# Attention kernel, two layers: both halves of P·V are copied out by ScalarE and added by GpSimd, instead of one copy and an addition on VectorE

## The chip, the cores and the metric

The kernel runs on one core of one Trainium2 chip. The metric is the device time of one execution in microseconds (us), as the median of the runs. TensorE is written PE (PEld for its weight loads), VectorE DVE, ScalarE ACT, GpSimd POOL, SyncE SP.

## The reference

Two attention layers over a batch of 8 images with 512 channels and T = 32·32 = 1024 positions, all float32; layer 1 has the same form with its own weights.

```python
xn = group_norm(x, w, b)                       # 32 groups
qkv = einsum('oc,bct->bot', qkv_w, xn) + qkv_b # 8 heads of 64 channels
weight = softmax(einsum('bct,bcs->bts', q * scale, k * scale), axis=-1)
a = einsum('bts,bcs->bct', weight, v)
hout = einsum('oc,bct->bot', proj_w, a) + proj_b
return x + hout
```

## The kernel before, in words

To hold float32 accuracy, each operand of a matmul is split into a rounded high part and the rest, the low part (`pt_hi` and `pt_lo`, `a_hi` and `a_lo`, and so on). Products of high and low parts are added up in PSUM.

The program is 16 passes (2 layers by 8 images). A pass has a head of its own (normalised input, queries, keys, values), then 4 **pairs** of heads, then the projection. A pair is 16 **steps** m = 0..15, one for each tile of 128 query rows. The first three pairs are a loop body ("middle pairs"); the last is written apart (`last=True`), since it has no next queries and keys to compute, and PE fills some of its steps with single matmuls of the projection. Every engine has its own instruction list, written out by hand and run in its order; semaphores tie the lists together. Nothing reorders them, so what stands behind a waiting instruction on an engine waits too.

What step m does:

- PE computes the scores of tile m+2 (`ps_s`, L766 and L768), transposes the normalised probabilities of tile m (`ps_t`, L777), computes a piece of the next head's queries and keys (middle pairs, L731), and does half of a **weigh** (`ps_o`, L789 and L790): the product of the values with the transposed probabilities of two tiles. The weigh of group k (k = 0..7) runs in steps 2k+2 and 2k+3; the weigh of group 7 stands behind step 15.
- DVE takes the row minimum of tile m+2 (L575), subtracts to get `pt_lo` of tile m (L584, two halves), and takes the reciprocal of the row sum of tile m+2 (L579).
- ACT copies `pt_hi` of tile m out of `ps_t` (`high_part`, L477, two halves) and computes the exponential of tile m+2 (L472).
- POOL multiplies tile m+2 by the reciprocal (`normalise`, L373), and splits queries, keys, values and weights for what comes next.

PE may transpose tile m only when tile m is normalised and `pt_lo` of tile m-1 is written (`lo_ready`, half by half).

The stationary operand of a weigh holds the high and the low values side by side, so that `ps_o` ends with two halves of 64 partitions that have to be added. ACT copies one half, shifted to the partitions of the other, into `o_part` (`other_half`, L484), and DVE adds it to the half that is still in PSUM, into `attn` (`add_halves`, L593). Groups 0 to 3 give the lower head, 4 to 7 the upper. When groups 4+k are in, `attn` is split: `attn_high(k)` on ACT (L497), `attn_split(k)` on POOL (L400). PE's next weigh waits for `attn_ready`, which says that `ps_o` has been read.

Where these stand: in a middle pair ACT does `other_half` at the start of even steps 4 to 14 and behind the high parts in step 15; in the last pair it stands in odd steps, between the high parts and the exponential. The end of a pair on ACT is `attn_high(2)`, `other_half` of group 7, `attn_high(3)`, and right behind it the high parts of tile 0 of the next pair.

Of the kernel before, what the change touches and what calls it, by code (L numbers as in the profile page):

```python
# [7 lines left out]
F32 = mybir.dt.float32  # L8
F32R = mybir.dt.float32r
I32 = mybir.dt.int32  # L10
ALU = mybir.AluOpType
# [25 lines left out]
LO_CREDIT, SUM_CREDIT, SPLIT_CREDIT, OUT_CREDIT, PV_CREDIT, STORE_CREDIT = 2, 1, 4, 8, 1, 1  # L37
# [10 lines left out]
def build(nc, x, wqk, wv, wp, bqk, bv, bo, nw, nb, consts, out):  # L48
    mid = nc.dram_tensor("layer0_out", (B, C, T), F32, kind="Internal").ap()

    with ExitStack() as ctx:
# [40 lines left out]
        o_part = [sb(f"o_part{s}", [P, GROUP], F32) for s in range(2)]  # L92
        a_hi = sb("a_hi", [P, PAIRS, T], F32R)
# [111 lines left out]
        def sum_at(g):  # L205
            return g + 1 + SUM_CREDIT

# [122 lines left out]
        def _(pool):  # L330
# [51 lines left out]
            nc.gpsimd.memset(scratch[:, 4:6], 0.0).then_inc(a_ready, SPLIT_CREDIT)  # L382
# [9 lines left out]
            split_wqk(1, 1, 0)  # L392

# [8 lines left out]
            def pair_steps(i, p, last):  # L402
                pair = PAIRS * i + p
                tile = TILES * i + PT_STEPS * p
                for e in range(2):
                    hh = 2 * p + e
                    hd = H * i + hh
                    for j in range(NT):
                        m = NT * e + j
                        if j == 1 and not (last and e == 1):  # L410
                            split_qk(hd + 1, 1 - e, 1)
                        if j == 3 and not (last and e == 1):
                            v_low(hd + 1, hh + 1, 1 - e)
                        if e == 1 and j in (5, 7):
                            attn_split(pair, p, (j - 5) // 2)
                        if j == 4 + e and not (last and e == 1):
                            split_wqk(hd + 3, 1 - e, pair + 1 + e)
                        if j == 6 and not last:
                            pool.wait_ge(scores_ready, tile + NT * (e + 1))
                            split_qk(hd + 2, e, 0)  # L420
                        if not (last and m + 2 >= PT_STEPS):
                            normalise(tile + m + 2, m + 2)
                attn_split(pair, p, 2)
                attn_split(pair, p, 3)
# [28 lines left out]
        def _(act):  # L453
# [26 lines left out]
            def other_half(g, k):  # L480

                src, dst = (slice(D, P), slice(0, D)) if k < 4 else (slice(0, D), slice(D, P))
                act.wait_ge(pv_done, pv_at(g))
                nc.scalar.copy(o_part[k % 2][dst, :], ps_o[src, 0:GROUP]).then_inc(part_ready, 1)  # L484
# [86 lines left out]
        def _(dve):  # L571
# [15 lines left out]
            def add_halves(pair, k):  # L587
                rows = slice(0, D) if k < 4 else slice(D, P)
                cols = slice((k % 4) * GROUP, (k % 4 + 1) * GROUP)
                dve.wait_ge(part_ready, 8 * pair + k + 1)  # L590
                if k < 4:
                    dve.wait_ge(a_ready, a_at(pair - 1, k))
                nc.vector.tensor_tensor(attn[rows, cols], ps_o[rows, 0:GROUP], o_part[k % 2][rows, :],  # L593
                                        ALU.add).then_inc(attn_ready, 1)

# [65 lines left out]
            nc.vector.memset(scratch[:, 1:2], 0.0).then_inc(attn_ready, SUM_CREDIT)  # L661
# [18 lines left out]
            def pair_steps(i, p, last):  # L680
                pair = PAIRS * i + p
                tile = TILES * i + PT_STEPS * p
                for m in range(PT_STEPS):
                    if not last and m >= 4 and m % 2 == 0:
                        add_halves(pair, m // 2 - 2)
# [4 lines left out]
                    if m == PT_STEPS - 1 or last and m >= 3 and m % 2 == 1:  # L690
                        add_halves(pair, (m - 3) // 2)
# [10 lines left out]
                add_halves(pair, 7)  # L702
# [24 lines left out]
        def _(pe):  # L727
# [53 lines left out]
            def weigh(tile, g, hd, k, lo, hi):  # L781

                if lo == 0:
                    pe.wait_ge(attn_ready, sum_at(g - 1))
                    pe.wait_ge(v_ready, hd + 1)
                    pe.wait_ge(lo_ready, lo_at(tile + 2 * k + 1, 1))
# [165 lines left out]
```

## Time and profile before

| | |
|---|---|
| median of 3 runs | 4327.01 us (4325.28 to 4327.69) |
| the profiled execution's own time | 4325.15 us |
| its span | 4323.0 us |
| PE busy | 4279.9 us, 99% |
| DVE busy | 3280.7 us, 76% |
| ACT busy | 2915.8 us, 67% |
| POOL busy | 2429.0 us, 56% |
| granted PE clock | 1.00 of full speed |

The profiled execution spends 2.15 us outside its span and lies 1.86 us below the median. A matmul's record includes its passage through the array, so records overlap; the distance from one start to the next tells more than their lengths. The chain of work that ended last gives each matmul only the time by which it moved that chain on.

### The profile page before, as it was taken

Reading aid. Unit: us, or ns where it says so; the run is one execution under the profiler, and the core shown is the slowest. Engines: PE = TensorE matmul, PEld = TensorE weight load, DVE = VectorE, ACT = ScalarE, POOL = GpSimd, SP = SyncE. Lnnn points to the kernel's source line nnn. Section 1 sums busy time; section 2 is a strip of 40 time slices with the busy share of each in tenths; the row PEclk is TensorE's granted clock in tenths of the full one; section 3 lists DMA queues with packets and bytes.
Section 4 is the critical chain, followed back from the end, with each engine's and each line's share of the span. In section 5 each row is a group of like instructions: output and inputs, shape, how many; then the busy total and the mean of one; then the engine's idle time right before and its main releaser. Section 6 shows DMA issues by size and latency. Waiting matters only on the chain.

```text
span 4323.0 us, 89926 instructions
## 1 busy us (share of the span) xinstructions
PE 4279.9 (99%) x26692; PEld 3740.2 (87%) x26692; DVE 3280.7 (76%) x5479; ACT 2915.8 (67%) x5375; POOL 2429.0 (56%) x2332
## 2 busy tenths in 40 slices
PE   8999999999999999999999999999999999999999
PEld 6888888888888888888888888888888888888888
DVE  5777867788686786777867788686886867868787
ACT  4757847577575775757757577575775757667576
POOL 5655556465564655646566465564655646556464
PEclk9999999999999999999999999999999999999999
DMA  3232222322223222232222212222222222222222
GB/s 87 49 96 47 71 72 49 96 47 80 64 47 96 48 79 65 49 94 49 78 74 60 86 45 83 64 63 81 47 81 66 65 79 48 79 64 68 75 49 88
DMA packets 99645, 295.08 MB, mean 68 GB/s; under 512 B 15104, under 2 KB 15232, under 8 KB 99328
## 3 DMA queue, kind: packets, MB, share of 16 engines
q1 hardware_dynamic: 99328, 291.19, 25.0%
q8 instruction: 158, 2.59, 0.2%
q14 instruction: 159, 1.30, 0.1%
HBM read 123.36 MB, written 33.55 MB: 36 GB/s over the span
## 4 chain that ended last, share of the span: by engine, by line
PE 97%; DVE 2%; issue 1%; ACT 0%; DMA 0%; DVEq 0%; POOL 0%; SPq 0%; POOLq 0%
PE ps_t L777 21%; PE ps_g L731 15%; PE ps_o L789 11%; PE ps_o L790 11%; PE ps_s L768 11%; PE ps_s L766 11%; PE ps_s L731 7%; PE ps_t L731 5%; PE ps_o L731 3%; DVE rstd_bits L627 0%; DVE seed L625 0%; DVE pt_lo L584 0%; ACT pt_hi L477 0%; DVE work L631 0%; DVE rstd_bits L632 0%
## 5 line engine op out<-in xcount | busy, mean ns | idle before, releaser
L373 POOL TENSOR_SCALAR probs<-probs,row_rcp 128x1024 f32<-128x1024 f32 x1024 | 1149.5, 1123 | 1371.1 <-DVE row_rcp L579 1371.1
L575 DVE TENSOR_REDUCE row_min<-ps_s 128x1 f32<-128x1024 f32 x1024 | 1250.4, 1221 | 214.4 <-PE ps_s L768 198.9
L477 ACT CAST pt_hi<-ps_t 128x512 fp32r<-128x512 f32 x2048 | 1112.0, 590 | 434.7 <-PE ps_t L777 423.5
L584 DVE TENSOR_TENSOR pt_lo<-ps_t,pt_hi 128x512 fp32r<-128x512 f32 x2048 | 1309.5, 680 | 9.5 <-ACT pt_hi L477 5.0
L472 ACT ACTIVATE probs<-ps_s,row_min 128x1024 f32<-128x1024 f32 x1024 | 1150.7, 1124 | 210.2 <-DVE row_min L575 193.6
L777 PEld LDWEIGHTS ps_t<-const_sb,probs 128*128 128x128 f32 x8192 | 945.2, 140 | 179.5 <-DVE pt_lo L584 49.6
L777 PE MATMUL ps_t<-const_sb,probs 128*128 128x128 f32 x8192 | 1084.1, 274 | 3.6 <-DVE pt_lo L584 3.4
L789 PE MATMUL ps_o<-pt_hi,v_st 128*128 128x256 f32 x4096 | 1044.2, 288 | 0.0
L790 PE MATMUL ps_o<-pt_lo,v_st 128*128 128x256 f32 x4096 | 1014.9, 282 | 0.0
L768 PE MATMUL ps_s<-kl_st,q_st 128*128 128x512 f32 x2048 | 808.7, 395 | 0.0
L766 PE MATMUL ps_s<-kh_st,q_st 128*128 128x512 f32 x2048 | 806.6, 394 | 0.0
L789 PEld LDWEIGHTS ps_o<-pt_hi,v_st 128*128 128x128 f32 x4096 | 771.9, 188 | 38.9 <-issue 12.4
L790 PEld LDWEIGHTS ps_o<-pt_lo,v_st 128*128 128x128 f32 x4096 | 774.6, 189 | 29.1
L768 PEld LDWEIGHTS ps_s<-kl_st,q_st 128*128 128x128 f32 x2048 | 388.1, 190 | 53.8
L593 DVE TENSOR_TENSOR attn<-ps_o,o_part 64x256 f32<-64x256 f32 x512 | 215.8, 421 | 281.2 <-ACT o_part L484 276.2
L766 PEld LDWEIGHTS ps_s<-kh_st,q_st 128*128 128x128 f32 x2048 | 385.9, 188 | 48.6
L731 PE MATMUL ps_g<-xn_hi,wqk_hi 128*128 128x512 f32 x768 | 352.7, 459 | 0.0
L362 POOL TENSOR_TENSOR kl_st<-qk,kh_st 128x512 fp32r<-128x512 f32 x256 | 329.3, 1286 | 21.4
L484 ACT COPY o_part<-ps_o 64x256 f32<-64x256 f32 x512 | 187.6, 366 | 186.4 <-PE ps_o L790 179.4
L731 PE MATMUL ps_g<-xn_hi,wqk_lo 128*128 128x512 f32 x768 | 307.2, 400 | 0.0
L579 DVE RECIPROCAL row_rcp<-row_sum 128x1 f32<-128x1 f32 x1024 | 167.9, 164 | 182.4 <-ACT probs L472 147.8
L400 POOL TENSOR_TENSOR a_lo<-attn,a_hi 128x256 f32 (+1 forms) x256 | 189.8, 741 | 204.3 <-ACT a_hi L497 204.3
(117 smaller groups left out, 4948.7 us busy)
## 6 DMA issues: line engine op xcount, KB each, us to landing
wqk_raw<-in_wqk SPq DMA_DIRECT2D x130, 256.0 KB, 2.6
q_st<-kh_st SPq DMA_DIRECT2D x128, 256.0 KB, 2.9
q_st<-kl_st SPq DMA_DIRECT2D x128, 256.0 KB, 3.6
kh_st<-kh_st SPq DMA_DIRECT2D x128, 256.0 KB, 2.9
kl_st<-kl_st SPq DMA_DIRECT2D x128, 256.0 KB, 3.6
x_raw<-layer_out SPq DMA_DIRECT2D x36, 512.0 KB, 5.3
wv_raw<-in_wv SPq DMA_DIRECT2D x66, 256.0 KB, 4.4
x_raw<-in_x SPq DMA_DIRECT2D x32, 512.0 KB, 5.3
```

Of the source, the lines that this page charges most:

```text
L362: nc.gpsimd.tensor_tensor(kl_st[s][:, cols], qk[:, cols], f32(kh_st[s][:, cols]), ALU.subtract).then_inc(qk_split, 1)
L373: nc.gpsimd.tensor_scalar(probs[m % 2][:, :], probs[m % 2][:, :], row_rcp[:, m % 4:m % 4 + 1], 1.0, ALU.mult, ALU.mult).then_inc(probs_rea ...
L472: nc.scalar.activation(probs[m % 2][:, :], ps_s[:, m % 2, :], ACT.Exp, bias=row_min[:, m % 4:m % 4 + 1], scale=-1.0, accum_out=row_sum[:, ...
L477: nc.scalar.copy(pt_hi[:, m // 2 % 2, 4 * half:4 * half + 4, (m % 2) * P:(m % 2 + 1) * P], ps_t[:, half, :].rearrange("p (b t) -> p b t", ...
L575: nc.vector.tensor_reduce(row_min[:, m % 4:m % 4 + 1], ps_s[:, m % 2, :], AX.X, ALU.min).then_inc(min_ready, 1)
L584: nc.vector.tensor_tensor(pt_lo[place], ps_t[:, half, :].rearrange("p (b t) -> p b t", b=4), f32(pt_hi[place]), ALU.subtract).then_inc(lo_ ...
L731: return nc.tensor.matmul(bank, stat[hi_lo[0]](n // 3), mov[hi_lo[1]](n // 3), start=first, stop=last)
L766: nc.tensor.matmul(ps_s[:, m % 2, cols], q_st[s][:, j * P:(j + 1) * P], kh_st[s][:, cols], start=True, stop=False)
L768: mm = nc.tensor.matmul(ps_s[:, m % 2, cols], q_st[s][:, j * P:(j + 1) * P], kl_st[s][:, cols], start=False, stop=True)
L777: mm = nc.tensor.transpose(ps_t[:, half, b * P:(b + 1) * P], probs[m % 2][:, (4 * half + b) * P:(4 * half + b + 1) * P], ident)
L789: nc.tensor.matmul(ps_o[:, 0:GROUP], v, pt_hi[:, k % 2, b, :], start=(b == 0), stop=False)
L790: mm = nc.tensor.matmul(ps_o[:, 0:GROUP], v, pt_lo[:, k % 2, b, :], start=False, stop=(b == BLK - 1))
```

## The change

ACT now makes two copies for each group: the half that stays on its partitions goes to a new buffer `o_same`, the other to `o_part` as before. POOL adds the two from SBUF into `attn`. PE's next weigh waits for ACT's second copy (`part_ready`), no longer for the addition. DVE's 512 additions are gone; the waits of `attn_high` and `attn_split` for `attn_ready` now wait for POOL.

```diff
+            def add_halves(pair, k):                       # block.gpsimd
+                rows = slice(0, D) if k < 4 else slice(D, P)
+                cols = slice((k % 4) * GROUP, (k % 4 + 1) * GROUP)
+                pool.wait_ge(part_ready, part_at(8 * pair + k))
+                if k < 4:
+                    pool.wait_ge(a_ready, a_at(pair - 1, k))
+                nc.gpsimd.tensor_tensor(attn[rows, cols], o_same[k % 2][rows, :], o_part[k % 2][rows, :],
+                                        ALU.add).then_inc(attn_ready, 1)
+                pool.wait_ge(attn_ready, sum_at(8 * pair + k))
...
                         m = NT * e + j
+                        if m >= 4 and m % 2 == 0:
+                            pool.wait_ge(probs_ready, tile + m + 2)
+                            add_halves(pair, m // 2 - 2)
...
+                if last:
+                    pool.wait_ge(a_ready, a_at(pair, 1))
+                else:
+                    pool.wait_ge(probs_ready, tile + PT_STEPS + 2)
+                add_halves(pair, 6)
                 attn_split(pair, p, 2)
+                pool.wait_ge(a_ready, a_at(pair, 2))
+                add_halves(pair, 7)
                 attn_split(pair, p, 3)
...
             def other_half(g, k):                          # block.scalar
+                act.wait_ge(attn_ready, sum_at(g - 2))
                 act.wait_ge(pv_done, pv_at(g))
+                nc.scalar.copy(o_same[k % 2][dst, :], ps_o[dst, 0:GROUP])
                 nc.scalar.copy(o_part[k % 2][dst, :], ps_o[src, 0:GROUP]).then_inc(part_ready, 1)
...
-            def add_halves(pair, k):                       # block.vector, with its three calls
-                dve.wait_ge(part_ready, 8 * pair + k + 1)
-                nc.vector.tensor_tensor(attn[rows, cols], ps_o[rows, 0:GROUP], o_part[k % 2][rows, :],
-                                        ALU.add).then_inc(attn_ready, 1)
...
             def weigh(tile, g, hd, k, lo, hi):             # block.tensor
                 if lo == 0:
-                    pe.wait_ge(attn_ready, sum_at(g - 1))
+                    pe.wait_ge(part_ready, part_at(g - 1))
```

The end of a middle pair on POOL, from the normalisation of tile 17 (tile 1 of the next pair) to the loop's end. Before:

```order
L373 TENSOR_SCALAR probs_81<-probs_81,row_rcp 128x1024 [waits rcp_ready]
L398 REGISTER_ALU
L399 REGISTER_ALU [waits attn_ready]
L400 ISA [waits a_hi_done]
L400 TENSOR_TENSOR a_lo<-attn,a_hi 128x256
L398 REGISTER_ALU
L399 REGISTER_ALU [waits attn_ready]
L400 ISA [waits a_hi_done]
L400 TENSOR_TENSOR a_lo<-attn,a_hi 128x256
```

And in the changed kernel, where L407 is the addition:

```order
L378 TENSOR_SCALAR probs_83<-probs_83,row_rcp 128x1024 [waits rcp_ready]
L407 TENSOR_TENSOR attn<-o_same_78,o_part_76 64x256 [waits part_ready,probs_ready]
L409 REGISTER_ALU
L416 REGISTER_ALU [waits attn_ready]
L417 ISA [waits a_hi_done]
L417 TENSOR_TENSOR a_lo<-attn,a_hi 128x256
L449 REGISTER_ALU
L407 TENSOR_TENSOR attn<-o_same_79,o_part_77 64x256 [waits part_ready,a_ready]
L409 REGISTER_ALU
L416 REGISTER_ALU [waits attn_ready]
L417 ISA [waits a_hi_done]
L417 TENSOR_TENSOR a_lo<-attn,a_hi 128x256
```

The additions of groups 6 and 7 stand behind that normalisation, each ahead of a subtraction of `a_lo`, and the second also waits for the first subtraction (`a_ready`).

The same place on ACT in the changed kernel, from the exponential of tile 17 (L499) on; before, the rows are the same but for L512 and its wait for `attn_ready`:

```order
L499 ACTIVATE probs_83,row_sum<-ps_s,row_min 128x1024 [waits transposed,min_ready]
L229 REGISTER_ALU [waits qk_split]
L486 ACTIVATE qk<-ps_g,bqk_sc,qk_scale 128x512 [waits qk_acc]
L525 REGISTER_ALU
L526 ISA [waits attn_ready]
L526 COPY a_hi<-attn 128x256
L512 COPY o_same_79<-ps_o 64x256 [waits pv_done,attn_ready]
L513 COPY o_part_77<-ps_o 64x256
L525 REGISTER_ALU
L526 ISA [waits attn_ready]
L526 COPY a_hi<-attn 128x256
```

The two copies of `a_hi` stand where they stood, but the semaphore that each waits for now comes from POOL.

An odd step of the last pair on ACT, changed kernel: the second high part (L504), the copies, the exponential (L499). Before there was one copy here, L484.

```order
L504 CAST pt_hi<-ps_t 128x4x128 [waits transposed]
L511 REGISTER_ALU [waits attn_ready]
L512 COPY o_same_79<-ps_o 64x256 [waits pv_done]
L513 COPY o_part_77<-ps_o 64x256
L496 REGISTER_ALU
L499 ACTIVATE probs_83,row_sum<-ps_s,row_min 128x1024 [waits transposed,min_ready]
```

What moved here is the exponential: it stands behind one more copy.

## Rows read from the trace of the kernel before

**Rows 1.** The page: busy us of each engine (share) x instructions.
```profile
PE 4279.9 (99%) x26692; PEld 3740.2 (87%) x26692; DVE 3280.7 (76%) x5479; ACT 2915.8 (67%) x5375; POOL 2429.0 (56%) x2332
```

**Rows 2.** The page: the chain that ended last, by engine.
```profile
PE 97%; DVE 2%; issue 1%; ACT 0%; DMA 0%; DVEq 0%; POOL 0%; SPq 0%; POOLq 0%
```

**Rows 3.** The waits of PEld: us in total, times, longest.
```profile
PEld ps_t L777 <- DVE pt_lo L584: 49.6, 213, 0.6
```

**Rows 4.** The page's groups: count | busy us, mean ns | idle before, releaser.
```profile
L593 DVE TENSOR_TENSOR attn<-ps_o,o_part 64x256 f32<-64x256 f32 x512 | 215.8, 421 | 281.2 <-ACT o_part L484 276.2
...
L484 ACT COPY o_part<-ps_o 64x256 f32<-64x256 f32 x512 | 187.6, 366 | 186.4 <-PE ps_o L790 179.4
...
L400 POOL TENSOR_TENSOR a_lo<-attn,a_hi 128x256 f32 (+1 forms) x256 | 189.8, 741 | 204.3 <-ACT a_hi L497 204.3
```

**Rows 5.** Timeline, a middle pair: normalisation of tile 6, its transposes (start, length).
```profile
76.84 1.13 POOL L373 TENSOR_SCALAR probs<-probs,row_rcp 128x1024 f32<-128x1024 f32 x1 [0.90 <-DVE row_rcp L579]
...
79.97 1.04 PE L777 MATMUL ps_t<-const_sb,probs 128*128 128x128 f32 x8
```

**Rows 6.** Timeline of ACT, end of the first middle pair.
```profile
114.46 0.39 ACT L497 CAST a_hi<-attn 128x256 f32 x1
...
116.65 0.41 ACT L497 CAST a_hi<-attn 128x256 f32 x1 [0.59 <-DVE attn L593]
117.15 1.07 ACT L477 CAST pt_hi<-ps_t 128x512 fp32r<-128x512 f32 x2
118.11 1.14 ACT L472 ACTIVATE probs<-ps_s,row_min 128x1024 f32<-128x1024 f32 x1
```

**Rows 7.** Timeline of POOL, the same place.
```profile
114.29 1.12 POOL L373 TENSOR_SCALAR probs<-probs,row_rcp 128x1024 f32<-128x1024 f32 x1 [1.21 <-DVE row_rcp L579]
...
117.24 0.74 POOL L400 TENSOR_TENSOR a_lo<-attn,a_hi 128x256 f32 x1 [1.12 <-ACT a_hi L497]
```

**Rows 8.** Timeline of DVE, steps 0 and 1 of the next pair.
```profile
119.36 0.16 DVE L579 RECIPROCAL row_rcp<-row_sum 128x1 f32<-128x1 f32 x1
...
120.60 1.28 DVE L584 TENSOR_TENSOR pt_lo<-ps_t,pt_hi 128x512 fp32r<-128x512 f32 x2
```

**Rows 9.** The chain, transposes of tile 2 there (start, us moved on).
```profile
121.60 0.99 PE ps_t L777 x8
```

**Rows 10.** Timeline of ACT, last pair, step 5.
```profile
243.07 0.37 ACT L484 COPY o_part<-ps_o 64x256 f32<-64x256 f32 x1 [0.36 <-PE ps_o L790]
243.46 1.12 ACT L472 ACTIVATE probs<-ps_s,row_min 128x1024 f32<-128x1024 f32 x1
```

**Rows 11.** Timeline of DVE, last pair, steps 5 and 6.
```profile
244.70 0.17 DVE L579 RECIPROCAL row_rcp<-row_sum 128x1 f32<-128x1 f32 x1 [0.41 <-ACT probs L472]
...
245.94 1.28 DVE L584 TENSOR_TENSOR pt_lo<-ps_t,pt_hi 128x512 fp32r<-128x512 f32 x2
```

**Rows 12.** The chain, last pair: transposes of tiles 6 and 7.
```profile
244.19 0.87 PE ps_t L777 x8
...
246.95 0.98 PE ps_t L777 x8
```

**Rows 13.** Timeline of POOL, last pair, step 4.
```profile
240.31 0.62 POOL L334 TENSOR_SCALAR wqk_hi<-wqk_raw 128x512 fp32r<-128x512 f32 x1
241.01 1.28 POOL L336 TENSOR_TENSOR wqk_lo<-wqk_raw,wqk_hi 128x512 fp32r<-128x512 f32 x1
242.26 1.13 POOL L373 TENSOR_SCALAR probs<-probs,row_rcp 128x1024 f32<-128x1024 f32 x1
```

**Rows 14.** Timeline, between two passes: POOL's last normalisation, ACT's copy of it.
```profile
286.81 6.77 POOL L379 TENSOR_SCALAR x_raw<-x_raw,norm_a,norm_b 128x1024 f32<-128x1024 f32 x4 [3.04 <-DVE norm_b L636]
...
293.62 1.05 ACT L488 CAST xn_hi<-x_raw 128x1024 fp32r<-128x1024 f32 x1 [1.08 <-POOL x_raw L379]
```

**Rows 15.** All groups of lines: one POOL operation beside DVE's L641, and alone.
```profile
L379 POOL TENSOR_SCALAR x_raw<-x_raw,norm_a,norm_b 128x1024 f32<-128x1024 f32 x60 | 101.9, 1714 | 45.5 <-DVE norm_b L636 45.5
...
L388 POOL TENSOR_SCALAR x_raw<-x_raw,norm_a,norm_b 128x1024 f32<-128x1024 f32 x2 | 2.4, 1189 | 4.6 <-DVE norm_b L636 4.6
```

More of the change, by code:

```diff
@@ L35 @@
 RSQRT_SEED = 0x5F3759DF
-LO_CREDIT, SUM_CREDIT, SPLIT_CREDIT, OUT_CREDIT, PV_CREDIT, STORE_CREDIT = 2, 1, 4, 8, 1, 1
+LO_CREDIT, SUM_CREDIT, SPLIT_CREDIT, OUT_CREDIT, PV_CREDIT, STORE_CREDIT = 2, 2, 4, 8, 1, 1
+PART_CREDIT = 1
 CHAIN = 20
@@ L92, in build @@
         o_part = [sb(f"o_part{s}", [P, GROUP], F32) for s in range(2)]
+        o_same = [sb(f"o_same{s}", [P, GROUP], F32) for s in range(2)]
         a_hi = sb("a_hi", [P, PAIRS, T], F32R)
@@ L206, in sum_at, with part_at @@
             return g + 1 + SUM_CREDIT
+        def part_at(g):
+            return g + 1 + PART_CREDIT
         def a_at(pair, k):
@@ L380, in x_normalise @@
                                         ALU.mult, ALU.add).then_inc(xn_f32, 1)
-            nc.gpsimd.memset(scratch[:, 4:6], 0.0).then_inc(a_ready, SPLIT_CREDIT)
+            nc.gpsimd.memset(scratch[:, 4:5], 0.0).then_inc(a_ready, SPLIT_CREDIT)
+            nc.gpsimd.memset(scratch[:, 5:6], 0.0).then_inc(attn_ready, SUM_CREDIT)
             nc.gpsimd.memset(scratch[:, 6:8], 0.0).then_inc(out_stored, STORE_CREDIT)
@@ L585, in low_part @@
                                         f32(pt_hi[place]), ALU.subtract).then_inc(lo_ready, 1)
-            def add_halves(pair, k):
-                rows = slice(0, D) if k < 4 else slice(D, P)
-                cols = slice((k % 4) * GROUP, (k % 4 + 1) * GROUP)
-                dve.wait_ge(part_ready, 8 * pair + k + 1)
-                if k < 4:
-                    dve.wait_ge(a_ready, a_at(pair - 1, k))
-                nc.vector.tensor_tensor(attn[rows, cols], ps_o[rows, 0:GROUP], o_part[k % 2][rows, :],
-                                        ALU.add).then_inc(attn_ready, 1)
             def half_stats(seq, c):
@@ L660, in _ @@
             nc.vector.memset(scratch[:, 0:1], 0.0).then_inc(lo_ready, LO_CREDIT)
-            nc.vector.memset(scratch[:, 1:2], 0.0).then_inc(attn_ready, SUM_CREDIT)
+            nc.vector.memset(scratch[:, 1:2], 0.0).then_inc(part_ready, PART_CREDIT)
             nc.vector.memset(scratch[:, 2:3], 0.0).then_inc(out_ready, OUT_CREDIT)
@@ L683, in pair_steps @@
                 for m in range(PT_STEPS):
-                    if not last and m >= 4 and m % 2 == 0:
-                        add_halves(pair, m // 2 - 2)
                     if not (last and m + 2 >= PT_STEPS):
@@ L689, in pair_steps @@
                     low_part(tile + m, m, 1)
-                    if m == PT_STEPS - 1 or last and m >= 3 and m % 2 == 1:
-                        add_halves(pair, (m - 3) // 2)
                     if not (last and m + 2 >= PT_STEPS):
@@ L701, in pair_steps @@
                     group_spread(i + 1)
-                add_halves(pair, 7)
             with dve.Fori(0, PASSES) as i:
```

## The prediction

> **What bounds the kernel.** I read the busy times first: PE is busy 99% of the time, the others 56 to 76% [rows 1]. The chain of work that ended last says the same: 97% of it is PE, 2% DVE [rows 2]. So the kernel is a PE kernel, and the change takes no instruction from PE. Work taken from DVE is worth only what PE waits for DVE. The waits of PEld give that: 49.6 us in 213 waits for `pt_lo` [rows 3]. They are not spread evenly. In the chain, eight transposes move it on by 0.87 us where nothing is late; tile 7 of the last pair took 0.98, and tile 2 of a middle pair 0.99 [rows 12, 9]. In these two places PE arrives with `pt_lo` only just there, so they have no slack left for anything that comes later than now. Elsewhere there is slack: in the first middle pair tile 6 is normalised from 76.84 to 77.97 and transposed from 79.97, with 2.0 us between [rows 5].
>
> **DVE's additions, removed.** 512 additions of 0.421 us, 215.8 us in all [rows 4]. Ahead of them DVE sat idle for 281.2 us, for ACT's copy. In the last pair the addition is followed by 0.41 us of idle time before the reciprocal, which waits for the exponential [rows 11]. So the addition stands in a hole on either side. Its removal lets the row minimum of an even step of a middle pair start up to 0.4 us earlier, and there the slack of 2.0 us makes that worth nothing. Gain: 0, at most a part of the 49.6 us.
>
> **The second copy.** Same shape as the first, 0.366 us [rows 4]; from the start of that copy in step 5 of the last pair to the start of the exponential behind it lie 0.39 us [rows 10]. I take 0.39 for one more copy. In even steps of a middle pair (groups 0 to 5) the high parts and so on move by 0.39 us at most, against 2.0 us of slack: 0. In the last pair it is another matter. There the copy stands ahead of the exponential of tile m+2, and the sequence closes on itself: weigh done, copy at 243.07, exponential from 243.46, reciprocal at 244.70 (released by ACT), DVE's minimum of the next tile, `pt_lo` of tile 6 from 245.94 to 247.22 [rows 10, 11], and PE's second four transposes of tile 7 wait for it, which is what stretched them to 0.98 from 0.87 [rows 12]; then comes the weigh that the next copy waits for. No member of the ring is idle for another reason, so 0.39 us in ACT is 0.39 us for each turn. The turns are the odd steps with an exponential behind the copy, m = 3, 5, 7, 9, 11, 13: six in a pass, 96 in all. **96 × 0.39 = 37 us.** If the ring had slack that the rows hide, the price would be 0.
>
> **The end of a middle pair.** This is the main term. `attn_high(2)` ran at 114.46 and `attn_high(3)` at 116.65, after the addition on DVE; ACT then went on with the high parts of the next pair's tile 0 at 117.15 [rows 6]. Now both wait for POOL, and all that is behind them on ACT waits too. Step by step, with these pieces: a handover from ACT to POOL 0.18 (ACT's 116.65 + 0.41 = 117.06, POOL at 117.24 [rows 6, 7]); from POOL to ACT 0.05 (286.81 + 6.77 = 293.58, ACT at 293.62 [rows 14]); POOL waiting for its own last result 0.08 (240.31 + 0.62 = 240.93, next at 241.01 [rows 13]). For the addition itself the trace has no row on POOL with 64 partitions. The nearest is `a_lo`, two inputs and 256 elements, on 128 partitions, at 0.741 us; DVE's own addition took 0.421 [rows 4]. I take 0.74, since DVE's rows show nothing of how long POOL needs; the lower end is 0.42, the upper end comes below.
>
> - The exponential of tile 17 starts 0.39 later behind the extra copy of group 6, so POOL's normalisation of it runs 114.68 to 115.80 instead of from 114.29 [rows 7].
> - Addition of group 6 behind it: 115.88 to 116.62.
> - `attn_high(2)` 116.67 to 117.07 instead of at 114.46.
> - Two copies of group 7: 117.10 to 117.85. Meanwhile `attn_split(2)` on POOL, 117.25 to 117.99.
> - Addition of group 7, which waits for both: 118.07 to 118.81.
> - `attn_high(3)` 118.86 to 119.26; high parts of tile 0 from 119.35, with the gap of 0.09 that was there. Before: 117.15. **2.20 us later.**
>
> Does PE feel all of it? ACT's exponential of tile 2 started right behind those high parts, at 118.11 [rows 6], and ended at 119.25; DVE's reciprocal at 119.36 waits for it, then come a minimum and `pt_lo` of tile 1 from 120.60 to 121.88 [rows 8], and PE's transposes of tile 2, from 121.60 on the chain, were already held by it (0.99 in place of 0.87 [rows 9]). So each link is direct and 2.20 us on ACT are 2.20 us on PE. From step 2 on, slack of about 2 us is back and nothing more is lost, nor can it be made good, since PE was the bound. There are 3 such ends in each of 16 passes: **48 × 2.20 = 106 us.**
>
> **Edits with no price.** PE's weigh waits for the second copy and not for the addition: the copy ends 0.39 later, the addition that it replaces took 0.42, so PE is released no later. The wait of the copies for the addition of two groups earlier was met some 7 us before. In step 4 of the last pair the addition stands ahead of a split of weights and the normalisation of tile 6, which ran at 242.26 [rows 13]: 0.39 + 0.74 + 0.16 later, it ends at 244.68, where the transposes of tile 6 moved the chain from 244.19 on [rows 12]. With the 0.39 of step 3 they would start at 244.58, so this costs about 0.1 to 0.3; but the next turn of the ring brings its 0.39 anyway and covers it. At the end of a pass ACT and POOL are late as well, but PE has 21 matmuls of the projection ahead of the last weigh: 0.
>
> **What a page says.** The Trainium skill, GPSIMD Engine Reference, section 3 ("Performance versus the Vector engine"), speaks against moving this work: an addition of two float32 tiles takes 1.96 times as long on GpSimd as on VectorE. By that ratio DVE's 0.421 us would be an estimated 0.825 on POOL, and each middle pair's end 0.17 us worse, 8 us in all. No row here times the same addition on both engines.
>
> **Sum.** 106 + 37 = 143 us on the profiled execution's 4325.15: 4468. The median of the runs lies 1.86 us above that execution, so I forecast 4470 us, 3.3% slower. A change of under 0.2% (9 us) could not be told from none by this measurement.
>
> **Rivals.**
>
> 1. *POOL's addition is lengthened by DVE.* The trace has such a case: POOL's normalisation of `x_raw` took 1.189 us alone and 1.714 beside DVE's L641, which reads two operands from SBUF [rows 15], a factor of 1.44. Then the addition takes 1.07, each pair's end 0.66 more: 48 × 0.66 = 32, and 4502 us. Against it: DVE's work at a pair's end takes one or both operands from PSUM, and `a_lo` took 0.741 beside it. The same page, section 1, names two SBUF inputs of VectorE as a case of contention; by that rule, the trace agrees, and the addition should stay at 0.74. Chance 0.12.
> 2. *The ring of the last pair absorbs the copy*, because DVE is free and PE's single fill matmuls leave room: only 106 us, 4433. Against it: the 0.98 in place of 0.87. Chance 0.10.
> 3. *The pair's end is cheaper.* An addition of 64 partitions at DVE's 0.42 takes 0.64 from each end, 31 us less: 4439. Chance 0.06.
> 4. *Not slower: DVE's relief decides.* PE's only waits in the pairs are for `pt_lo` from DVE, 49.6 us [rows 3]. If the additions were what made `pt_lo` late, their removal would end those waits and the kernel would take some 4275. That needs POOL to hand its sums over so early that ACT's high parts at 117.15 come less than (49.6 - 37) / 48 = 0.26 us later. Against it: DVE is idle before and after the additions [rows 4, 11], and two additions and a subtraction on POOL, 2.2 us, now stand between the exponential and ACT. Chance 0.06, half of it faster, half within 0.2%.
>
> **How the numbers follow.** The forecast has 0.66. Its own range comes from the handovers and the addition: 4455 to 4490. To leave out no more than 2 in 10 the range must take in rivals 1 to 3: 4430 to 4508. Faster 0.03, same 0.03, slower 0.94.
>
> **What would show it.** In the profile after: DVE busy down by some 216 us, ACT up by 187, POOL up by 512 × 0.74 = 379. The addition's mean says which of 0.42, 0.74 and 1.07 holds. At a middle pair's end ACT waits for `attn` from POOL ahead of both copies of `a_hi`, and the high parts come at about 119.3 plus what was lost before. PE's wait for `pt_lo` grows from 49.6 to some 190 us, in transposes of tiles 1 and 2, and the steps in the middle of a middle pair keep their length. In the last pair two steps take 0.39 us longer than before. I would be wrong if the steps in the middle of a pair grew (POOL then has no slack there), or if PE went through the pair's end without a wait.

## The result, and the profile after

The changed kernel takes 4510.56 us (median of 5 runs, 4508.99 to 4510.73) against 4327.01 us: ratio 1.0426, 95% interval 1.0414 to 1.0438. It is 183.6 us slower. The forecast said slower by 143 us, 4470 us, with a range to 4508; the time lies 2.6 us above that range.

The page of the changed kernel: busy times and the chain by engine, to be read beside [rows 1, 2].

```profile
span 4506.9 us, 91335 instructions
...
PE 4339.2 (96%) x26692; PEld 3771.4 (84%) x26692; DVE 3098.0 (69%) x4967; ACT 3058.1 (68%) x5887; POOL 2809.0 (62%) x2845
...
PE 79%; issue 6%; ACT 5%; POOL 5%; DVE 4%; ACTq 1%; POOLq 0%; DVEq 0%; DMA 0%; SPq 0%
```

POOL is busy for 380 us more, as forecast (379). DVE is busy for 183 us less and ACT for 142 more, where the forecast had 216 and 187: the instructions taken away and added are as long as forecast (215.8 and 187.8 us), but a busy time counts a moment once when two instructions of an engine overlap in it.

Before, 97% of the chain was PE. Now ACT, POOL, DVE and the handovers between them ("issue") hold a fifth of it: work that lay beside PE has come onto the path. The groups that answer to [rows 3, 4]:

```profile
L407 POOL TENSOR_TENSOR attn<-o_same,o_part 64x256 f32<-64x256 f32 x512 | 375.6, 734 | 161.2 <-ACT o_part L513 92.7
...
L512 ACT COPY o_same<-ps_o 64x256 f32<-64x256 f32 x512 | 187.8, 367 | 130.5 <-PE ps_o L805 126.4
```

And of its waits (sum in us, number, longest in us):

```profile
PEld ps_t L792 <- DVE pt_lo L613: 215.5, 285, 2.6
```

The addition takes 0.734 us on POOL, a copy 0.367. PEld's wait for `pt_lo` has grown from 49.6 to 215.5 us, and its longest from 0.6 to 2.6 us.

**The end of a middle pair.** First ACT in the changed kernel, the place of [rows 6] (PE and ACT come to the pair's last step 2.01 us later here, from the start of the kernel on):

```profile
118.79 0.41 ACT L526 CAST a_hi<-attn 128x256 f32 x1 [1.79 <-POOL attn L407]
119.22 0.37 ACT L512 COPY o_same<-ps_o 64x256 f32<-64x256 f32 x1
119.60 0.36 ACT L513 COPY o_part<-ps_o 64x256 f32<-64x256 f32 x1
121.07 0.40 ACT L526 CAST a_hi<-attn 128x256 f32 x1 [1.10 <-POOL attn L407]
121.56 1.07 ACT L504 CAST pt_hi<-ps_t 128x512 fp32r<-128x512 f32 x2
```

ACT sits idle for 1.79 us ahead of the first copy of `a_hi` and for 1.10 us ahead of the second, both times for POOL. The high parts of tile 0 come at 121.56; without the change they would have come at 117.15 + 2.01 = 119.16. That is 2.40 us late (forecast: 2.20). DVE and PE at the same place:

```profile
122.18 1.29 DVE L613 TENSOR_TENSOR pt_lo<-ps_t,pt_hi 128x512 fp32r<-128x512 f32 x2 [2.42 <-ACT pt_hi L504]
...
122.93 1.25 PE L792 MATMUL ps_t<-const_sb,probs 128*128 128x128 f32 x8 [1.94 <-DVE pt_lo L613]
```

DVE waits 2.42 us for ACT, PE 1.94 us for DVE, ahead of the transposes of tile 1.

**Step by step against before.** The table is worked out from the two traces: for each tile the end of its last transpose, changed kernel less kernel before, and how much that difference grows from one tile to the next, in us, as a mean over passes 1 to 15.

```
tile            0     1     2     3     4     5     6     7     8     9    10    11    12    13    14    15
pair 0       0.28  0     0     0     0     0     0     0     0     0     0     0     0     0     0     0
pair 1      -0.10  2.87  0.70  0     0     0     0     0     0     0     0     0     0     0     0     0
pair 2      -0.10  2.37  0.23  0     0     0     0     0     0     0     0     0     0     0     0     0
pair 3      -0.10  2.58  0.13 -0.02  0     0.38  0.89 -0.11  0     0.38  0     0.38  0     0.28  0     0.44
```

Everything is lost in two places: tiles 1 and 2 of pairs 1 to 3, behind the end of a middle pair (135.6 us in all), and the last pair from tile 5 on (42.0 us). The rest is 4.2 us at tile 0 of pair 0, between passes, and 2.0 us once before the first tile; the sum is 183.8. In the middle of a middle pair nothing is lost. But the 135.6 us are 2.83 for each of 48 ends, not 2.40. The ends come in two kinds: 25 cost 2.38 us on average, 23 cost 3.31.

**What sets the 23 apart** is PE's clock. The windows of the changed kernel around the end of pair 0 in pass 1 (columns: length, busy us of each engine with counts, granted clock, DMA):

```profile
398.00:400.00 2.00, 1.33 (x6) 0.75 (x4) 0.10 (x1) 0.79 (x3) 1.21 (x2) 1.00 0.00 0
400.00:402.00 2.00, 0.71 (x5) 0.61 (x6) 1.29 (x2) 2.00 (x4) 0.72 (x1) 0.89 0.00 0
402.00:404.00 2.00, 2.00 (x8) 1.81 (x8) 1.87 (x4) 1.62 (x5) 1.50 (x2) 0.50 0.00 0
404.00:406.00 2.00, 2.00 (x11) 1.57 (x11) 1.16 (x4) 0.76 (x2) 1.92 (x3) 0.75 0.00 0
```

And PE in that stretch:

```profile
401.29 1.74 PE L792 MATMUL ps_t<-const_sb,probs 128*128 128x128 f32 x8 [1.96 <-DVE pt_lo L613]
402.68 0.78 PE L746 MATMUL ps_g<-xn_hi,wqk_hi 128*128 128x512 f32 x1
403.25 0.63 PE L746 MATMUL ps_g<-xn_lo,wqk_hi 128*128 128x512 f32 x1
```

PE was idle for 1.96 us, then its granted clock is 0.50, the 1.2 GHz level, and matmuls that move on by 0.23 us elsewhere move on by 0.43. The record of the granted clock has 23 such stretches within the work of the changed kernel, one at each of the 23 ends, and none within that of the kernel before. They cost 23 × (3.31 - 2.38) = 21 us: about 1.1 us at each of the 15 that lie at the first or second end of a pass, 0.6 at the 8 at a third end.

**The last pair.** The chain of the changed kernel through step 4 of the first last pair (start, us moved on):

```profile
248.74 1.13 POOL probs L378
...
250.14 0.72 POOL attn L407
...
251.15 0.62 POOL wqk_hi L339
...
253.12 1.13 POOL probs L378
...
254.37 1.09 PE ps_t L792 x8
```

POOL normalises tile 5, adds group 0, splits weights, normalises tile 6, and PE waits for that. Between 249.87 and 250.14, and between 250.86 and 251.15, POOL does nothing but pass waits, among them one for its own last result each time: 0.27 and 0.29 us.

### The profile page after: what moved, and what is told of

Its sections match the earlier page's. It is cut to its first block, busy times and chain, and to the rows that moved or that the text cites. A ratio compares the mean times of both kernels' runs of the same rounds, so it can differ in the third digit from the quotient of the medians.

```text
span 4506.9 us, 91335 instructions
## 1 busy us (share of the span) xinstructions
PE 4339.2 (96%) x26692; PEld 3771.4 (84%) x26692; DVE 3098.0 (69%) x4967; ACT 3058.1 (68%) x5887; POOL 2809.0 (62%) x2845
## 4 chain that ended last, share of the span: by engine, by line
PE 79%; issue 6%; ACT 5%; POOL 5%; DVE 4%; ACTq 1%; POOLq 0%; DVEq 0%; DMA 0%; SPq 0%
PE ps_t L792 18%; PE ps_g L746 12%; PE ps_o L805 9%; PE ps_o L804 9%; PE ps_s L783 8%; PE ps_s L781 8%; PE ps_s L746 7%; PE ps_t L746 5%; PE ps_o L746 3%; ACT probs L499 3%; POOL probs L378 2%; POOL attn L407 2%; DVE pt_lo L613 1%; ACT o_part L513 1%; ACT pt_hi L504 1%
## 5 line engine op out<-in xcount | busy, mean ns | idle before, releaser
L504 ACT CAST pt_hi<-ps_t 128x512 fp32r<-128x512 f32 x2048 | 1113.6, 590 | 452.6 <-PE ps_t L792 436.6
L499 ACT ACTIVATE probs<-ps_s,row_min 128x1024 f32<-128x1024 f32 x1024 | 1153.7, 1127 | 146.0 <-DVE row_min L604 138.3
L792 PEld LDWEIGHTS ps_t<-const_sb,probs 128*128 128x128 f32 x8192 | 954.6, 142 | 330.7 <-DVE pt_lo L613 215.5
L792 PE MATMUL ps_t<-const_sb,probs 128*128 128x128 f32 x8192 | 1107.8, 277 | 122.8 <-DVE pt_lo L613 101.0
L407 POOL TENSOR_TENSOR attn<-o_same,o_part 64x256 f32<-64x256 f32 x512 | 375.6, 734 | 161.2 <-ACT o_part L513 92.7
L746 PE MATMUL ps_g<-xn_lo,wqk_hi 128*128 128x512 f32 x768 | 307.8, 401 | 0.0
L512 ACT COPY o_same<-ps_o 64x256 f32<-64x256 f32 x512 | 187.8, 367 | 130.5 <-PE ps_o L805 126.4
```

The lines of the kernel that those rows point to most:

```text
L407: nc.gpsimd.tensor_tensor(attn[rows, cols], o_same[k % 2][rows, :], o_part[k % 2][rows, :], ALU.add).then_inc(attn_ready, 1)
L499: nc.scalar.activation(probs[m % 2][:, :], ps_s[:, m % 2, :], ACT.Exp, bias=row_min[:, m % 4:m % 4 + 1], scale=-1.0, accum_out=row_sum[:, ...
L504: nc.scalar.copy(pt_hi[:, m // 2 % 2, 4 * half:4 * half + 4, (m % 2) * P:(m % 2 + 1) * P], ps_t[:, half, :].rearrange("p (b t) -> p b t", ...
L746: return nc.tensor.matmul(bank, stat[hi_lo[0]](n // 3), mov[hi_lo[1]](n // 3), start=first, stop=last)
L792: mm = nc.tensor.transpose(ps_t[:, half, b * P:(b + 1) * P], probs[m % 2][:, (4 * half + b) * P:(4 * half + b + 1) * P], ident)
```

## The experiments

All are timed against the kernel before on the same chip, in 4 to 10 runs. The time is the median of the runs; the rest is read from the one execution that was profiled. "An end" is the loss at tiles 0 to 3 behind the end of a middle pair, and "falls" are stretches at half clock; both are read as above.

| kernel | us | ratio (95%) | an end | falls | last pair, tiles 4 to 15, 16 passes |
|---|---|---|---|---|---|
| changed | 4510.56 | 1.0426 (1.0414 to 1.0438) | 2.83 | 23 | 42.0 |
| e1, extra copy | 4402.36 | 1.0175 (1.0158 to 1.0192) | 0.50 | 0 | 36.7 |
| e2b, half addition | 4455.77 | 1.0300 (1.0284 to 1.0316) | 1.90 | 3 | 37.8 |
| e3, copies behind exponential | 4453.69 | 1.0294 (1.0276 to 1.0311) | 2.71 | 15 | -6.6 |
| e4, order at the end | 4416.85 | 1.0208 (1.0191 to 1.0225) | 0.94 | 0 | 42.4 |
| e5, before, ACT later | 4356.77 | 1.0071 (1.0054 to 1.0088) | 0.48 | 0 | 0.5 |
| e6, before, ACT later still | 4405.57 | 1.0185 (1.0168 to 1.0202) | 1.53 | 0 | -0.1 |
| e10, before, as late as the change | 4456.95 | 1.0304 (1.0288 to 1.0320) | 2.49 | 7 | 0.2 |
| e7, deferred high parts | 4365.30 | 1.0092 (1.0075 to 1.0109) | -0.14 | 0 | 42.0 |
| e8, e7 and e3 | 4318.14 | 0.9982 (0.9973 to 0.9992) | -0.14 | 0 | -3.8 |
| e9, before with e3's move | 4332.39 | 1.0014 (1.0004 to 1.0023) | 0.00 | 0 | 5.7 |
| e11, e8 and a split behind | 4313.77 | 0.9971 (0.9960 to 0.9981) | -0.15 | 0 | -9.5 |

**e1: the second copy alone.** To the kernel before:

```diff
                 act.wait_ge(pv_done, pv_at(g))
+                nc.scalar.copy(o_same[k % 2][dst, :], ps_o[dst, 0:GROUP])
                 nc.scalar.copy(o_part[k % 2][dst, :], ps_o[src, 0:GROUP]).then_inc(part_ready, 1)
```

> The kernel before, with the extra ScalarE copy into o_same that nothing reads; the additions stay on VectorE. Theory of the ring: each of 96 odd steps of the last pairs grows by 0.38 us (36 us), and each of 48 middle pairs' ends by one copy, since the addition on VectorE and with it the last high part of attn come 0.39 us later (48 x 0.39 = 19 us): 4327 + 55 = 4382 us. Rival, that what the last pair lost came from GpSimd's order (additions and splits ahead of the normalisations) and not from the copy: only the ends' 19 us, about 4346 us. Rival, that a copy on ScalarE is hidden everywhere: 4327 us.

75 us slower. The last pair loses 36.7 us, 0.38 at each of tiles 5, 7, 9, 11, 13 and 15, as the ring wants it. The ends lose 0.50 each, 24 us. What was not expected is 0.32 us at tile 13 of every middle pair, 15.6 us: with DVE still adding, ACT's extra copy is felt there too. The addition of group 4, in the kernel before and in e1:

```profile
101.11 0.43 DVE L593 TENSOR_TENSOR attn<-ps_o,o_part 64x256 f32<-64x256 f32 x1 [0.90 <-ACT o_part L484]
...
100.96 0.43 DVE L595 TENSOR_TENSOR attn<-ps_o,o_part 64x256 f32<-64x256 f32 x1 [1.28 <-ACT o_part L486]
```

It waits 0.38 us longer for ACT, and the minimum of tile 14 and `pt_lo` of tile 12 behind it on DVE come later by as much, for which PE's transposes of tile 13 wait. In the changed kernel no addition stands ahead of them, and nothing is lost at that tile. So the relief of DVE was worth 15.6 us after all, but only against a loss that the change itself brings.

**e2 and e2b: the length of the addition.** The first form (e2) gave no time: it leaves half of `attn` unwritten, and that half is read later. The second, to the changed kernel, sets `attn` to zero once at the start; both leave out half of the sums:

```diff
-            nc.gpsimd.memset(scratch[:, 5:6], 0.0).then_inc(attn_ready, SUM_CREDIT)
+            nc.gpsimd.memset(attn[:, :], 0.0).then_inc(attn_ready, SUM_CREDIT)
...
-                nc.gpsimd.tensor_tensor(attn[rows, cols], o_same[k % 2][rows, :], o_part[k % 2][rows, :],
+                part = slice((k % 4) * GROUP, (k % 4) * GROUP + P)
+                nc.gpsimd.tensor_tensor(attn[rows, part], o_same[k % 2][rows, 0:P], o_part[k % 2][rows, 0:P],
```

> The changed kernel with every addition on GpSimd over 128 of the 256 columns; the other half of the sums is left out. The addition should take some 0.42 us instead of 0.734. Theory, that each end of a middle pair costs the sum of its steps and that TensorE falls to half clock where it then idles for about 2 us: each end is 2 x 0.31 = 0.62 us shorter, 30 us, and with the shorter idle time all or most of the 22 us of the clock go too: 4458 to 4480 us. Rival, that the 22 us have nothing to do with how long TensorE idles: 4480 us, with as many stretches at half clock as in the changed kernel. Rival, that the handovers and not the addition set the time: 4510 us.

> The changed kernel with every addition on GpSimd over 128 of the 256 columns (the other half of the sums is left out, attn is set to zero once at the start). The addition should take about 0.42 us instead of 0.734. Theory: each of 48 ends is 2 x 0.31 = 0.62 us shorter, 30 us, and as TensorE then idles for about 1.3 us there in place of 1.96, there are few or no stretches at half clock, which gives back up to 22 us: 4458 to 4480 us. Rival, that the clock falls for another reason: 4480 us with about 23 such stretches. Rival, that the handovers and not the addition set the time: 4510 us.

The half addition, its group on POOL:

```profile
L408 POOL TENSOR_TENSOR attn<-o_same,o_part 64x128 f32<-64x128 f32 x512 | 234.5, 458 | 169.8 <-ACT o_part L514 101.4 <-POOL probs L378 49.9
```

And PE at the first end of a middle pair:

```profile
121.99 1.25 PE L793 MATMUL ps_t<-const_sb,probs 128*128 128x128 f32 x8 [1.40 <-DVE pt_lo L614]
```

0.276 us less for each addition, and ends without a fall cost 1.86 in place of 2.38 us: 0.52, close to two additions. PE idles for 1.40 to 1.43 us at the first two ends of a pass and for 1.68 at the third, and there are 3 falls in place of 23, all at third ends. 55 us faster than the changed kernel, a little more than the 52 of the theory's far end.

**e3: the copies off the ring.** To the changed kernel, in the last pair only:

```diff
-                        if m == PT_STEPS - 1 or last and m >= 3 and m % 2 == 1:
+                        if m == PT_STEPS - 1 and not last:
                             other_half(8 * pair + (m - 3) // 2, (m - 3) // 2)
                         if not (last and m + 2 >= PT_STEPS):
                             exponential(tile + m + 2, m + 2, 2 * (tile + m) + 2)
+                        if last and m >= 3 and m % 2 == 1:
+                            other_half(8 * pair + (m - 3) // 2, (m - 3) // 2)
```

> The changed kernel with ScalarE's two copies in the odd steps of the last pair moved from ahead of the exponential to behind it. Theory of the ring (weigh, copies, exponential, reciprocal, minimum, low part, transposes, weigh): the copies leave the ring, and the last pairs lose nothing against the kernel before and may gain the 0.1 us by which six transposes were stretched there: 4510 - 42 = 4468, down to 4458 us. If late normalisation of tile 6 on GpSimd alone sets something, some 6 us of it stay: 4474 us. Rival, that the weigh two steps on, which waits for the copies, is now late instead: within 10 us of 4510.

57 us faster. The last pair goes from +42.0 to -6.6: the ring is what cost it, and even the old 0.1 us of stretch is gone (-0.11 at tiles 5, 7, 9 and 11). Of the other 8 us the traces put 5.6 down to fewer falls, 15 in place of 23, though the ends were not touched; the rest is the difference between one execution and another. The rival, a late weigh, falls.

**e4: another order at the end.** To the changed kernel, middle pairs only: ACT copies group 7 out and then makes both high parts; POOL adds both groups and then subtracts. (The last pair keeps its order; the branch for it is not shown.)

```diff
-                attn_high(pair, p, 2)
                 other_half(8 * pair + 7, 7)
+                attn_high(pair, p, 2)
                 attn_high(pair, p, 3)
...
                 add_halves(pair, 6)
-                attn_split(pair, p, 2)
-                pool.wait_ge(a_ready, a_at(pair, 2))
                 add_halves(pair, 7)
+                attn_split(pair, p, 2)
                 attn_split(pair, p, 3)
```

> The changed kernel with the end of a middle pair in another order: ScalarE copies group 7 out first and then makes both high parts, GpSimd does both additions before both subtractions. By the durations of the trace the high parts of the next pair's tile 0 then come about 1.0 us late instead of 2.35. Theory: each of 48 ends costs 1.0 to 1.1 us instead of 2.42, 64 us less, and as TensorE then idles for well under 1 us, the clock stays up and 22 us more are saved: 4424 us. Rival, that the stretches at half clock come anyway: 4446 us. Rival, that the chain through the pair's end is not what TensorE waits for: 4510 us.

ACT and PE there:

```profile
115.92 0.40 ACT L530 CAST a_hi<-attn 128x256 f32 x1 [0.45 <-POOL attn L407]
116.73 0.41 ACT L530 CAST a_hi<-attn 128x256 f32 x1 [0.41 <-POOL attn L407]
...
118.59 1.25 PE L800 MATMUL ps_t<-const_sb,probs 128*128 128x128 f32 x8 [0.48 <-DVE pt_lo L621]
```

94 us faster, with the same instructions. ACT waits 0.86 us for POOL in place of 2.89, PE idles for 0.48 us at this end, and the clock never falls.

**e5, e6, e10: the same lateness without the additions on GpSimd.** To the kernel before, at the end of each middle pair, behind the last high part of `attn`, copies on ACT that nobody reads: three, seven or eleven (shown as in e5; in e10 the small ones are written as bf16).

```diff
                 attn_high(pair, p, 3)
+                if not last:
+                    for d in range(3):          # e6: 5, e10: 9
+                        nc.scalar.copy(dump[:, d, :], const_sb[:, 0:152])
+                    for d in range(2):          # e6 and e10
+                        nc.scalar.copy(o_part[d][:, :], const_sb[:, :])
```

> The kernel before with three small idle copies on ScalarE at the end of each of the 48 middle pairs, ahead of the high parts of the next tile 0: about 0.95 us more there, and GpSimd and the additions untouched. Theory, that whatever makes these high parts late is paid by TensorE in full, and that its clock holds over idle time of about 0.7 us: 48 x 0.95 = 46 us, 4373 us, no stretch at half clock. Rival, that the slack there hides most of it: under 4350 us.

> The same with seven idle copies, about 2.4 us at each of the 48 ends, as much as the change costs there. Theory: 48 x 2.4 = 115 us and, with TensorE idle for about 2 us at each, some twenty stretches at half clock that cost about 22 us together: 4464 us. Rival, that the clock falls in the changed kernel for another reason (GpSimd's or ScalarE's extra work): 4442 us and no stretch at half clock. That would leave the pair's end itself as the explanation of 115 us only.

> The kernel before with eleven idle copies on ScalarE at the end of each of the 48 middle pairs, so that the high parts of the next tile 0 come about 2.4 us late and TensorE idles for about 2 us, as in the changed kernel; the same kernel with 1.5 us showed no stretch at half clock. Theory, that the idle time alone brings TensorE's clock down: 48 x 2.4 = 115 us and some 10 to 25 stretches at half clock, 10 to 22 us more: 4452 to 4464 us. Rival, that the clock falls from the extra work on GpSimd and ScalarE: 4442 us and no such stretch.

The copies were shorter than reckoned (0.22 us from one to the next, the wider ones 0.30), so the lateness was smaller too: in e6 the high parts came at 118.02 behind a last copy of `a_hi` at 116.00, 1.52 us more than the 0.50 between the two in [rows 6], and an end cost 1.53. In e5 it was 0.97 less 0.50 and 0.48. So ACT's lateness is PE's loss, one for one, with none of the additions on GpSimd in it. The clock held in both, which by e6's own expectation spoke for its rival, but in e6 PE had idled for 0.95 to 1.41 us only. e10 brings ACT's lateness to the change's own, 2.40 us, and ends without a fall cost 2.40 us. A window at one of its 7 falls:

```profile
1342.00:1344.00 2.00, 2.00 (x9) 1.71 (x8) 2.00 (x3) 1.63 (x3) 1.76 (x3) 0.50 0.00 1
```

PE at that end, the third of its pass, and at the first end of pass 0, where the clock stayed:

```profile
1340.95 1.97 PE L783 MATMUL ps_t<-const_sb,probs 128*128 128x128 f32 x8 [2.27 <-DVE pt_lo L590]
...
120.59 1.25 PE L783 MATMUL ps_t<-const_sb,probs 128*128 128x128 f32 x8 [1.83 <-DVE pt_lo L590]
```

All 7 falls are at third ends, which idle for 2.27 us; the first two of each pass idle for 1.83, 0.1 less than in the changed kernel, where PE comes to them 0.10 earlier.

So PE's idle time brings falls without the additions on GpSimd and without the second copies. Counted by the idle time ahead of the transposes of tile 1:

```
kernel     ends 1 and 2 of a pass (32)     third end (16)
e4         0.47 to 0.52 us, no fall        0.76 to 0.78 us, no fall
e6         0.95 us, no fall                1.41 us, no fall
e2b        1.40 to 1.43 us, no fall        1.68 us, 3 falls
e10        1.82 to 1.83 us, no fall                2.27 us, 7 falls
changed    1.93 to 1.97 us, 15 falls       2.21 us, 8 falls
```

Longer idle times bring more of them, but length alone does not decide: 1.68 us brought 3 in e2b, and 1.83 us none of 32 in e10. These counts hold for one execution of each kernel. The other three of e10 took 4455.97 to 4458.17 us at a mean granted clock of 0.995 to 0.996, the profiled one 4452.84 us at 0.997, so they had more falls, and at which ends is not recorded.

**e7 and e8: ACT no longer waits for POOL at the end.** To the changed kernel: the loop body of ACT and POOL now runs from step 3 of one pair to step 2 of the next, which lets the last high parts of `attn` stand among the next pair's steps. Nothing is left out. On ACT, shortened:

```diff
-                attn_high(pair, p, 2)
-                other_half(8 * pair + 7, 7)
-                attn_high(pair, p, 3)
+                other_half(8 * pair + 7, 7)
+                pair_steps(i, p + 1, False, 0, 3, (2, 3))   # steps 0 to 2 of the next pair, with
+                                                            # attn_high(2) behind step 0, (3) behind step 1
```

POOL adds groups 6 and 7, does the next pair's steps 0 and 1, subtracts group 6, does step 2, subtracts group 7. e8 has e3's move as well.

> The changed kernel with the waits for GpSimd taken off ScalarE's path at the end of a middle pair: the copies of group 7 first, then the next pair's tile 0 (high parts, exponential of tile 2), and only behind these and the exponential of tile 3 the two high parts of attn; GpSimd adds both groups, goes on with the next tiles, and subtracts later. Nothing is left out. Theory: the ends cost under 0.4 us each and the clock stays up, what is left is the last pairs' 42 us and some 6: 4375 us, up to 4395. Rival, that GpSimd now has too much ahead of its normalisations of tiles 2 and 3 (one more addition, 0.74 us): 4400 to 4420 us.

> Both repairs, the deferred high parts and the copies behind the exponential in the last pair. Theory: 4375 - 42, to 4333 us, and if the 0.1 us of the six stretched transposes is gained, 4323 us. So VectorE's relief of 216 us of work brings at most 0.1% even where nothing stands in its way. Rival, that VectorE's relief was worth more and only covered by the waits: under 4300 us.

ACT in e8, at the end of the first middle pair and behind it:

```profile
116.61 1.07 ACT L515 CAST pt_hi<-ps_t 128x512 fp32r<-128x512 f32 x2 [0.62 <-PE ps_t L816]
...
118.67 0.41 ACT L537 CAST a_hi<-attn 128x256 f32 x1
```

The high parts of tile 0 wait for PE alone, and the copy of `a_hi` for nothing. An end now costs -0.14 us, and e8 is faster than the kernel before, by 0.18%. The rival of e7, that POOL has too much to do in the next pair's first steps, falls.

**e9: the same move without the change of engines.** To the kernel before, e3's move on ACT and, on DVE in the last pair, the addition behind the reciprocal:

> The kernel before with one thing moved: in the odd steps of the last pairs ScalarE's copy goes behind the exponential, and VectorE's addition behind the reciprocal. Theory, that the copy is part of a ring that stretched six transposes by 0.1 us in each last pair: 10 us less, 4317 us, without any change of engine. Then the two repaired kernels (this and the one with the additions on GpSimd) are alike, and the relief of VectorE brought nothing. Rival, that here the addition on VectorE now makes its minimum and low part late, so that nothing is gained or some is lost: 4327 us or more.

It got 6 us slower, not 10 faster: the rival was right. With the addition on DVE, the minimum and the low part behind it come late, up to 0.2 us a tile. The repaired kernel with the additions on GpSimd, e8, is 14 us faster than this one. So my theory that the relief of DVE brought nothing falls. How much of the 14 us is the relief is not shown: e8 also has the deferred high parts and PE's earlier release, and no run gives these to a kernel that adds on DVE.

**e11: the split behind the normalisation.** To e8, in step 4 of the last pair on POOL:

```diff
-                        if j == 4 + e and not (last and e == 1):
+                        if j == 4 + e and not last:
                             split_wqk(hd + 3, 1 - e, pair + 1 + e)
...
                             normalise(tile + m + 2, m + 2)
+                        if last and m == 4:
+                            split_wqk(hd + 3, 1 - e, pair + 1 + e)
```

> The changed kernel with both repairs (deferred high parts, copies behind the exponential) and, in step 4 of the last pairs, the split of weights on GpSimd behind the normalisation of tile 6 instead of ahead of it. Theory, that the addition ahead of that split makes tile 6 late by 0.4 us in each pass: 16 x 0.4 = 6 us under the 4318 of the kernel with the two repairs, 4312 us. Rival, that it costs nothing there, since the next step takes it up: 4318 us.

4.4 us less than e8, and in the trace tile 6 goes from +0.36 to 0, which is 5.7 us of 16 last pairs. The two ratios lie close together (their intervals overlap), so it is the trace that tells the two apart. It is the fastest kernel of the study, 0.29% faster than the one before.

## Why the prediction was right and where it was wrong

The direction and both mechanisms were right, and each was shown by its own experiment; the sum was 41 us short. The step that failed is that the end of a pair costs PE its stall and nothing behind it: PE's clock fell behind 23 of the 48 stalls, 21 us, half of what was missing. Without these the time would be 4489 us, inside the forecast's own range of 4455 to 4490. Term by term:

- **The second copy in the last pair**, forecast 96 × 0.39 = 37 us: 36.7 us in e1, and gone in e3. Right.
- **The end of a middle pair**, forecast 2.20 us: 2.38 at full clock, 9 us too little over 48 ends. The addition was right (0.734 for 0.74), and so was POOL's wait for its own last result (0.08). The handovers were not: from POOL's result to ACT's start lie 0.12 us, twice, where I took 0.05 from a row between passes, and the exponential of tile 17 starts 0.44 later in place of 0.39, since ACT's first copy ahead of it starts 0.06 later behind PE (0.37 us of idle time for 0.31). That PE feels it one for one is what e5, e6 and e10 show.
- **The clock**, not in the sum at all: 21 us. The forecast took PE's time behind the stall as unchanged ("From step 2 on, slack of about 2 us is back and nothing more is lost"). I had a stall of 2 us on a PE that had not idled for as much as 0.6 us within the pairs, and no row of the trace before shows what its clock does then; e2b, e4 and e10 do. Nor did a rival cover it.
- **"Edits with no price": tile 6 of the last pair.** I reckoned 0.1 to 0.3 us and thought the next turn of the ring would cover it. It cost 0.4 in each of 16 passes, 6 us, on top of the ring's own (tiles 6 and 7 together grew by 0.78 in place of 0.38); as tile 13 grew by 0.28 only, the last pairs took 42.0 us in all, 5 more than forecast. POOL's waits for its own result took 0.27 and 0.29 us where I had taken 0.08, and PE was then later than the ring. e11 removes it. On such waits the Trainium skill, GPSIMD Engine Reference, section 2.1 ("Instruction dispatch"), says that one Pool instruction does not hold back the next, and asks for a wait on the semaphore where an instruction reads partitions that another of the engine's cores wrote. No run here leaves such a wait out.
- **DVE's relief**, forecast 0. In the changed kernel it offsets 15.6 us that the second copy would cost in the middle pairs (e1). Another 5 us, the -0.10 at each tile 0 behind an end, come from PE's release and not from DVE's free time: before, the weigh of group 7 waits at all 48 ends, and starts 0.13 us behind the end of the addition of group 6 (first end: 113.48 behind 112.92 + 0.43); with the release by ACT's second copy that wait and its row are gone. In e1 it is 0.41 us long in place of 0.26, and tile 0 loses 0.15. The row of before, for which the profile names no releaser:

```profile
PEld ps_o L789 <- issue: 12.4, 48, 0.3
```

A net gain is left only when ACT's waits are gone (e8, 8 us under the kernel before and 14 under e9).
- **Small rest.** 4.2 us between passes and 2.0 at the start. Such amounts stand in most of the traces, with either sign at the start (-0.9 to +2.4 us), and were not looked into.

Sum: 143 + 9 + 21 + 5 + 6 = 184, measured 184. Of the rivals, the lengthened addition falls (0.734 us), and so do the absorbed copy, the cheap addition and the one in which DVE's relief decides. The ratio of the additions on the two engines is 0.734 / 0.421 = 1.74, with one operand of DVE's in PSUM. The Trainium skill, GPSIMD Engine Reference, section 3 ("Performance versus the Vector engine"), has 1.96 for 2048 elements: the right side, and too high for the 256 here.

What stays open: which ends bring the clock down. In the changed kernel 15 of 32 idle times of 1.95 us did and 17 did not, and 8 of 16 of 2.21 us: in each pass but the first one of its first two ends, and in 8 passes the third. e3, with the same ends and shorter last pairs, had 15 falls, some of them at other ends of the same passes. So the moment at which an end comes counts beside its length; by what rule, no experiment tells. Nor does one show falls behind 1.95 us without the change's extra work on GpSimd and ScalarE: the falls of e10 are behind 2.27 us.

## What to carry to other kernels

An engine with a third of its time free can still be on the path: what counts is whether its result is waited for by an in-order engine whose next instruction the bottleneck needs. When work is handed to a third engine, walk the handovers at the places where the bottleneck has no slack (here the first steps of a loop body and a ring of four engines), and move the instruction that waits behind the one that is needed; that, not the choice of engine, turned +4.3% into -0.3%. A stall of about 2 us on TensorE may cost more than its own length, since the clock can fall behind it (here 0.5 to 1.1 us more, at about half of such stalls in the changed kernel).

## What the runs showed of the hardware

- TensorE's granted clock fell to 0.50 behind idle times of 1.68 to 2.27 us, at 3 (e2b) to 23 (changed kernel) of 48 ends, and at no end of these traces that idled for 1.43 us or less. A fall cost 1.1 us more than the stall at the first two ends of a pass and 0.5 to 0.8 at the third.
- A GpSimd instruction that waits for GpSimd's own last result starts 0.08 to 0.30 us after it: in the changed kernel 0.08 for the additions of groups 4 and 5 of every pair and 6 and 7 of the middle pairs, 0.16 for groups 1 to 3, whose list has one more wait there, and 0.27 to 0.30 for group 0, the first of a pair.
- From a GpSimd result to the start of the ScalarE instruction that waited for it lay 0.12 us at the 48 ends of the changed kernel.
- GpSimd's two-input addition of 64 partitions took 0.734 us for 256 elements and 0.458 (e2b) for 128; its subtraction on 128 partitions and 256 elements took 0.738. So half the partitions save nothing, and half the elements save 38%.
